# Quantised cross attention in a six-stage transformer kernel: the transposes of 37 of 64 units of probabilities go from TensorE to DMA

## The reference

```python
q = (x @ Wq + bq).reshape(1, B * N, H, hd)            # 512 tokens, 16 heads of 16
kv = (cond @ Wkv + bkv).reshape(1, -1, 2, H, hd)      # 1024 keys
...
q = _fq_sym(q, axis=-1)
k = _fq_sym(k, axis=-1)
v = _fq_sym(v, axis=2)
attn = jnp.einsum('bhqd,bhkd->bhqk', q, k)
attn = jax.nn.softmax(attn.astype(jnp.float32), axis=-1)
attn = _fq_unsigned(attn, axis=-1)                    # rounded to 0..255 steps of its row's maximum
out = jnp.einsum('bhqk,bhkd->bhqd', attn, v)
out = jnp.transpose(out, (0, 2, 1, 3)).reshape(B, N, C)
return out @ Wp + bp
```

## Time and profile before

| what | us |
|---|---|
| three runs | 521.48, 514.76, 516.54; median 516.54 |
| the profiled execution, its whole time | 514.3 |
| its span in the trace | 512.4 |

### The profile page before, as it was taken

How to read it: one execution, slowest core, us unless ns; L and a number is a source line. 1 busy time by engine, 2 the same in 40 slices (tenths; PEclk the granted TensorE clock), 3 DMA queues, 4 the chain that set the end, 5 groups by cost and what they waited for, 6 DMA issues and landing times.

```text
span 512.4 us, 7879 instructions
## 1 busy us (share of the span) xinstructions
PE 447.2 (87%) x2922; PEld 287.7 (56%) x2959; DVE 323.0 (63%) x617; ACT 226.4 (44%) x546; POOL 101.1 (20%) x205
## 2 busy tenths in 40 slices
PE   4977979999996979999974599999999699899994
PEld 1354556666664536756653266666666454455563
DVE  1997368473624258787864789999999464122235
ACT  3331321122222366586520599989898532001000
POOL 6396042424225200000007011111111000000002
PEclk9998988999998879999998589999999989999998
DMA  8930000000000000000000340000000310312121
GB/s 294 317 92 2 0 0 1 0 2 1 1 0 0 1 0 2 2 1 2 1 1 0 123 207 2 1 3 1 2 1 2 117 50 10 123 44 60 41 61 42
DMA packets 12053, 20.63 MB, mean 40 GB/s; under 512 B 1576, under 2 KB 8552, under 8 KB 11688
## 3 DMA queue, kind: packets, MB, share of 16 engines
q1 hardware_dynamic: 12016, 20.14, 11.6%
HBM read 19.48 MB, written 0.66 MB: 39 GB/s over the span
## 4 chain that ended last, share of the span: by engine, by line
PE 72%; DVE 14%; ACT 6%; issue 6%; DMA 1%; POOL 1%; POOLq 0%; SPq 0%; DVEq 0%; ACTq 0%
PE ps L641 23%; PE ps L791 6%; PE ps L1043 5%; PE ps L830 5%; PE ps L841 4%; PE ps L755 4%; PE ps L940 4%; PE ps L960 4%; PE ps L949 4%; PE ps L762 4%; DVE area_a L1381 2%; ACT area_b L572 2%; PE ps L860 2%; PE ps L824 2%; DVE stats L1130 2%
## 5 line engine op out<-in xcount | busy, mean ns | idle before, releaser
L1381 DVE CUSTOM_DVE_ANT_0 area_a<-ps,zero,small 128x1024 f32<-128x1024 f32 x64 | 80.0, 1272 | 1.3 <-PE ps L940 1.3
L572 ACT ACTIVATE area_b<-area_a,small 128x1024 int16<-128x1024 f32 x64 | 72.9, 1142 | 5.9 <-POOL small L451 5.7
L553 ACT ACTIVATE area_a<-ps,small 128x256 f32<-128x256 f32 (+1 forms) x128 | 51.8, 434 | 31.1 <-DVE small L1273 28.8
L641 PE MATMUL ps<-xT_odd,area_a 128*128 128x512 f32 x128 | 58.3, 602 | 0.0
L400 POOL TENSOR_SCALAR var_eps<-meanvar 128x1 f32<-128x1 f32 x24 | 5.9, 245 | 239.5 <-DVE meanvar L1131 239.1
L1448 DVE TENSOR_TENSOR area_b<-ps,area_b 128x512 f32<-128x512 f32 x16 | 11.0, 690 | 52.8 <-ACT area_b L616 52.8
L949 PEld LDWEIGHTS ps<-ident_b,area_b 128*128 128x128 bf16 x512 | 34.0, 99 | 17.5 <-ACT area_b L572 5.3
L940 PE MATMUL ps<-area_b 128*128 128x512 bf16 x107 | 35.9, 405 | 7.5 <-DVE small L1381 3.5
L960 PE MATMUL ps<-area_a,area_b 128*32 128x128 bf16 x512 | 40.1, 222 | 1.0 <-ACT area_a L590 0.8
L1273 DVE TENSOR_REDUCE small<-ps 128x4 f32<-128x1024 f32 (+1 forms) x24 | 29.3, 1222 | 18.3 <-PE ps L830 18.1
L949 PE MATMUL ps<-ident_b,area_b 128*128 128x128 bf16 x512 | 40.0, 222 | 0.8 <-ACT area_b L572 0.7
(11 more groups left out here) (245 smaller groups left out, 789.5 us busy)
## 6 DMA issues: line engine op xcount, KB each, us to landing
area_a<-in_w_up_dram SPq DMA_DIRECT2D x1, 4096.0 KB, 13.6
area_b<-gates_out SPq DMA_DIRECT2D x16, 256.0 KB, 3.0
area_a<-in_w_down_dram SPq DMA_DIRECT2D x1, 2048.0 KB, 8.2
area_b<-in_idx_row_dram SPq DMA_DIRECT2D x1, 1024.0 KB, 7.5
ctxT<-in_ctxT_dram SPq DMA_DIRECT2D x1, 1024.0 KB, 9.5
ctx_tok<-in_ctx_dram SPq DMA_DIRECT2D x1, 1024.0 KB, 12.6
w_qkv<-in_w_qkv_dram SPq DMA_DIRECT2D x1, 768.0 KB, 6.2
xT_even<-in_xT_dram SPq DMA_DIRECT2D x1, 512.0 KB, 3.9
```

The source lines that it names most:

```text
L553: a = act.activation(p1[:, n % 2, x * nk * P:(x + 1) * nk * P], scores1(n)[:, x * nk * P:(x + 1) * nk * P], ACT.Exp, bias=nmx1[:, n % 2, x ...
L572: act.activation(px[:, u % PX, :], sx[:, u % 3, :], ACT.Exp, bias=nbx[:, u:u + 1], accum_out=zx[:, i, h:h + 1]).then_inc(sem("px_ready"), 1)
L641: mm = pe.matmul(dst, lhsT(c), rhs(c), start=start and c == 0, stop=stop and c == DC - 1, **kw)
L1381: dve.tensor_tensor_reduce(sx[:, u % 3, :], bank(2 * (u % 2), 2), zero[:].broadcast_to([P, B * M]), qsc[:, u // HX, u % HX:u % HX + 1], LO ...
```

## The change

37 of the 64 units, the ones whose conversion is DVE's, are no longer transposed by PE. SP issues one `dma_start_transpose` for each of them. It reads `px` in SBUF and writes `turned`, also in SBUF, which has three buffers of int16 and a semaphore for each. DVE then converts from `turned` and no longer from PSUM. The 27 units of ACT keep their path.

- `pTx` gets four buffers, two of them in another area, and a buffer is free again when `apply` of unit u-4 is done.
- On PE, `apply` is three units behind the transposes (before: one). On DVE, the conversion is one unit later in the order: maximum of u+3, then conversion of u.
- The exponential of unit u waits for the landing of the transfer of unit u-3 where that unit is one of the 37 (`px_turned`).
- Steps at the end of a tile (`turn_z`, `spread_z`, `project`, `normalise`, `add`, `norm_scale`, `evac_sums`, `evac_z`) come two or three units later.
- The semaphores `x_ready1` to `x_ready6` become one, `x_ready`, that counts on, and `xT_ready` likewise.

```diff
@@ -54,7 +54,7 @@
 SHARE = ((1, 3, 5), 7)
 TURN_AT = 1
 VALUES_AT = (5, 11)
-NORM_AT = 11
+NORM_AT = 14
 
 
 def build(nc, t, out):
@@ -216,7 +216,9 @@
         zx, rzx = tiny([TT, HX]), tiny([TT, HX])
 
         sx = carve("a", DC * E1 * 2 * HE, [3, B * M])
-        pTx = carve("a", DC * E1 * 2 * HE + 3 * B * M, [2, KT * P], BF16)
+        pTx = [carve(where, at + k * KT * P // 2, [KT * P], BF16)
+               for where, at in (("a", DC * E1 * 2 * HE + 3 * B * M), ("b", 26 * N)) for k in range(2)]
+        turned = carve("b", 11 * N, [3, KT * P], I16)
 
         w_up = carve("a", 0, [DC, 2, E1 * HE])
         w_down = carve("a", DC * E1 * 2 * HE, [NG, D])
@@ -250,10 +252,22 @@
 
             return u % SHARE[1] in SHARE[0]
 
+        def before5(u, by_act):
+
+            return sum(by_scalar(k) == by_act for k in range(u))
+
+        def px_turned(eng, u):
+
+            if by_scalar(u):
+                eng.wait_ge(sem("pTx_ps"), before5(u + 1, True))
+            else:
+                n = before5(u, False)
+                eng.wait_ge(sem(f"turned_{n % 3}"), 16 * (n // 3 + 1))
+
         def pTx_ready(eng, u):
 
             by_act = by_scalar(u)
-            eng.wait_ge(sem("pTx_act" if by_act else "pTx_dve"), sum(by_scalar(k) == by_act for k in range(u + 1)))
+            eng.wait_ge(sem("pTx_act" if by_act else "pTx_dve"), before5(u + 1, by_act))
 
         items1 = [(i, c, hh, gp) for i in range(TT) for c in range(DC) for hh in range(1 + i % 2) for gp in range(2)]
         first1 = [next(n for n, x in enumerate(items1) if x[0] == i) for i in range(TT)] + [len(items1)]
@@ -320,6 +334,16 @@
                 sp.wait_ge(sem("qTx_ps"), HX // 2)
                 load("w_up", w_up.rearrange("p c k h -> p (c k h)"), t["w_up"])
 
+                for u in range(TT * HX):
+                    if not by_scalar(u):
+                        n = before5(u, False)
+                        sp.wait_ge(sem("px_ready"), u + 1)
+                        if n >= 3:
+
+                            sp.wait_ge(sem("pTx_dve"), n - 2)
+                        sp.dma_start_transpose(out=turned[:, n % 3, :].rearrange("p (k q) -> p k q", k=KT),
+                                               in_=px[:, u % PX, :]).then_inc(sem(f"turned_{n % 3}"), 16)
+
                 sp.wait_ge(sem("px_ready"), TT * HX)
                 sp.wait_ge(sem("ox_ps"), TT * HX)
                 load("w_down", w_down, t["w_down"].rearrange("(g p) d -> p g d", p=P))
@@ -335,7 +359,7 @@
                     sp.dma_start(gate_rows[:, g % 4, :], rows).then_inc(sem(f"gate_rows_{g % 4}"), 16)
 
             for i in range(TT):
-                sp.wait_ge(sem(f"x_ready{STAGES}"), i + 1)
+                sp.wait_ge(sem("x_ready"), nth(STAGES, i))
                 sp.dma_start(out[i * P:(i + 1) * P, :], x_tok[STAGES % 2][:, i, :]).then_inc(sem("out_done"), 16)
             sp.wait_ge(sem("out_done"), 16 * TT)
 
...
@@ -568,14 +592,14 @@
                     act.wait_ge(sem("biasx_ready"), u + 1)
                     if u >= PX:
 
-                        act.wait_ge(sem("pTx_ps"), u - PX + 1)
+                        px_turned(act, u - PX)
                     act.activation(px[:, u % PX, :], sx[:, u % 3, :], ACT.Exp, bias=nbx[:, u:u + 1],
                                    accum_out=zx[:, i, h:h + 1]).then_inc(sem("px_ready"), 1)
                     if u and by_scalar(u - 1):
                         evac_px(u - 1)
-                    if h == 1 and i:
+                    if h == 4 and i:
                         evac_sums(i - 1)
-                    if h == 4 and i:
+                    if h == 6 and i:
                         evac_z(i - 1)
                 if by_scalar(TT * HX - 1):
                     evac_px(TT * HX - 1)
@@ -583,11 +607,12 @@
                 evac_z(TT - 1)
 
             def evac_px(u):
-                act.wait_ge(sem("pTx_ps"), u + 1)
-                if u >= 2:
-                    act.wait_ge(sem("ox_ps"), u - 1)
-
-                act.activation(pTx[:, u % 2, :], bank(4 + u % 2).bitcast(I16), ACT.Copy).then_inc(sem("pTx_act"), 1)
+                n = before5(u + 1, True)
+                act.wait_ge(sem("pTx_ps"), n)
+                if u >= 4:
+                    act.wait_ge(sem("ox_ps"), u - 3)
+
+                act.activation(pTx[u % 4], bank(4 + n % 2).bitcast(I16), ACT.Copy).then_inc(sem("pTx_act"), 1)
 
             def evac_sums(i):
 
...
@@ -942,11 +967,14 @@
                     mm.then_inc(sem("sx_ps"), 1)
 
                 def turn(u):
+                    if not by_scalar(u):
+                        return
+                    n = before5(u + 1, True)
                     pe.wait_ge(sem("px_ready"), u + 1)
-                    if u >= 2:
-                        pTx_ready(pe, u - 2)
+                    if n > 2:
+                        pe.wait_ge(sem("pTx_act"), n - 2)
                     for k in range(KT):
-                        mm = pe.transpose(bank(4 + u % 2).bitcast(BF16)[:, k * P:(k + 1) * P],
+                        mm = pe.transpose(bank(4 + n % 2).bitcast(BF16)[:, k * P:(k + 1) * P],
                                           px[:, u % PX, k * P:(k + 1) * P].bitcast(BF16), ident_b[:])
                     mm.then_inc(sem("pTx_ps"), 1)
 
@@ -957,7 +985,7 @@
                     c, pair = divmod(h // 2, P // PAIR)
                     dst = bank(6 + i % 2)[pair * PAIR:(pair + 1) * PAIR, c * P:(c + 1) * P]
                     for k in range(KT):
-                        mm = pe.matmul(dst, ivh[:, k * HX + h, :], pTx[:, u % 2, k * P:(k + 1) * P],
+                        mm = pe.matmul(dst, ivh[:, k * HX + h, :], pTx[u % 4][:, k * P:(k + 1) * P],
                                        start=h % 2 == 0 and k == 0, stop=h % 2 == 1 and k == KT - 1)
                     mm.then_inc(sem("ox_ps"), 1)
 
@@ -982,22 +1010,22 @@
                 pe.wait_ge(sem("in_stage5"), 4 * 16)
                 for u in range(3):
                     scores(u)
-                for u in range(units + 1):
+                for u in range(units + 3):
                     if u + 3 < units:
                         scores(u + 3)
                     if u < units:
                         turn(u)
-                    if u > HX and u % HX == 3:
+                    if u > HX and u % HX == 5:
                         turn_z(u // HX - 1)
-                    if u > HX and u % HX == 5:
+                    if u > HX and u % HX == 7:
                         spread_z(u // HX - 1)
-                    if u > HX and u % HX == 7:
+                    if u > HX and u % HX == 9:
                         project(u // HX - 1)
-                    if u % HX == 1 and u > 2 * HX:
+                    if u % HX == 3 and u > 2 * HX and u < units:
 
                         pe.wait_ge(sem("res5_ready"), u // HX - 1)
-                    if u:
-                        apply(u - 1)
+                    if u >= 3:
+                        apply(u - 3)
                 turn_z(TT - 1)
                 spread_z(TT - 1)
                 project(TT - 1)
...
@@ -1134,7 +1162,7 @@
 
                 dve.wait_ge(sem("rstd_ready"), nth(n, i))
                 TS(x_tok[n % 2][:, i, :], res[:, i, :], meanvar[:, i, 0:1], rstd[:, i:i + 1],
-                   ALU.subtract, ALU.mult).then_inc(sem(f"x_ready{n}"), 1)
+                   ALU.subtract, ALU.mult).then_inc(sem("x_ready"), 1)
 
             def norm(n, residual):
 
@@ -1383,11 +1411,11 @@
                                              mxx[:, u:u + 1]).then_inc(sem("maxx_ready"), 1)
 
                 def evacuate(u):
-                    dve.wait_ge(sem("pTx_ps"), u + 1)
-                    if u >= 2:
-                        dve.wait_ge(sem("ox_ps"), u - 1)
-
-                    dve.tensor_copy(pTx[:, u % 2, :], bank(4 + u % 2).bitcast(I16)).then_inc(sem("pTx_dve"), 1)
+                    px_turned(dve, u)
+                    if u >= 4:
+                        dve.wait_ge(sem("ox_ps"), u - 3)
+
+                    dve.tensor_copy(pTx[u % 4], turned[:, before5(u, False) % 3, :]).then_inc(sem("pTx_dve"), 1)
 
                 def invert_z(i):
                     dve.wait_ge(sem("px_ready"), HX * (i + 1))
@@ -1407,18 +1435,18 @@
                 units = TT * HX
                 maximum(0)
                 maximum(1)
-                for u in range(units):
+                for u in range(units + 1):
                     if u + 2 < units:
                         maximum(u + 2)
-                    if not by_scalar(u):
-                        evacuate(u)
-                    if u >= HX:
+                    if u and not by_scalar(u - 1):
+                        evacuate(u - 1)
+                    if u >= HX and u < units:
                         i = u // HX - 1
                         if u % HX == 1:
                             invert_z(i)
-                        if u % HX == 6:
+                        if u % HX == 9:
                             normalise(i)
-                        if u % HX == 8:
```

(1 more changed line is left out.)

26 lines of the change are left out of this document (13 added, 13 removed).

## The result

The changed kernel took 532.81 us, median of four runs (531.0 to 536.33), against 515.65 for the kernel before. The ratio is **1.036, 95% interval 1.028 to 1.044**: slower by about 17 us. The ratio is one of means and leaves out one execution of the kernel before (521.48 us) which ran in a slower state of the chip, so it is larger than the quotient of the two medians. On another chip, in a later group of runs, the ratio was 1.029 (1.024 to 1.035). The profiled execution has a span of 531.8 us, 19.4 more than before.

A forecast was written before the change was run, and what follows sets the result against it. No engine alone was taken to bound the loop (PE, DVE, ACT over 93% full). 306.7 + 128.9 + 1.23 + 5.15 + 7.68 = 449.7 us for the stage's end, +39.2; with 514.3 and 2.2 about 555 us, range 518 to 640.

The forecast's parts named there:

- the sign: Whole kernel: slower than before, chance 0.83; about 555 us against a median of 516.5.
- the three places of the loss: Start: exponential of unit 3 at 306.7 for 298.94; loop: 2.15 us a unit for 1.70; end: L for 0.72.
- the term L: From the exponential's end until `turned` can be read: between 3.0 and 7.3 us, taken as 5.15.
- everything else: Part of the gate rows' 3.0 us landing that is not service: 2.2 us, beside some 0.8 of service.
- the prediction's own formula: Loop through the landing: seven units take at least 2L + 4.74 us, overtaking the old pace from L = 3.6.
- The pace: Loop over the units: 2.15 us for a unit at L = 5.15, against 1.70 before.
- The ceiling of the gain: Loop from unit 3 to 63: can shrink only to ACT's 95.4 us, at most 6.5 us or 1.3%.
- The start: First transfer queues behind the 4 MB w_up: exponential of unit 3 at 306.7 us in place of 298.94.
- The end: After unit 63's exponential: L replaces the 0.72 us before its conversion; the last norm still ends 7.68 us later.
- The clock: TensorE's half clock at the start may last longer through waiting: nothing in the sum, 3 us in the range.
- the rival with L = 3.0 (524): Transfers land like a plain copy, service 0.8, engines keep 1.70 us a unit: +7.8, 524 us; chance 0.22.
- The conversion: DVE's conversion reading SBUF instead of PSUM: 0.69 us taken as the value, 414 ns as the lower bound.

The follow-up runs named there:

- late conversion: Changed kernel with DVE's conversion of unit u one unit later, after the maximum of u+4 instead of u+3: 525.31 us, ratio 1.019.
- The mended kernel: Changed kernel with w_up in 16 pieces, DVE's conversion one unit later, four px buffers, last three units on PE: 511.7 us, ratio 0.984; again 511.64 us, 0.988.

## Why the prediction was wrong

**What was right**: the sign, the three places of the loss, and ACT as the bound once the rest is mended. **The step that failed** is the term L, the landing. It read: "Nothing in the trace prefers an end; I take the middle, service 2.95 and L = 5.15 us". Measured were 1.63 us of service and a landing of 3.1. Two of its parts were sized wrong. The number of pieces was right (1056, against 1024), but each was charged 79 ns, the mean of a queue whose packets hold 1.7 KB: packets of 256 bytes took 25 ns. And the 2.2 us of "everything else" were 1.5, for the measured service with those 2.2 would have made 3.8. That one value carried 27 of the 39 us through the loop, and some 2 more at either end.

By the prediction's own formula an L of 3.1 gives (6.2 + 4.74) / 7 = 1.56 us a unit, under the 1.70 of before: on average the loop no longer sets the pace, and units 3 to 59 took 1.73. The formula says that a landing under 3.6 us costs nothing there, and that is not so either. With the same order and no transfers they took 92.1 us, so the landings cost 4.8, in single waits of DVE of up to 1.1 us each.

Point by point:

- **The pace**: 2.15 forecast, 1.73 measured for units 3 to 59. The formula is sound where the landing is as long as was assumed: 2.12 by it and 2.21 measured when every transfer was issued twice. In the changed kernel what holds is DVE's order (late conversion, 4.0 us); a fourth buffer of px changed nothing by itself.
- **The ceiling of the gain**: I had seen that ACT leaves 6.5 us at most, of the 101.9 from unit 3 to unit 63. The mended kernel took 98.4 and 98.1 in its two traces, which is 3.5 to 3.8 of them, and the kernel with all units on PE 100.3. The changed kernel took 107.0. DVE's conversions, shorter by 37 x 0.26 = 9.7 us in all, came back as waits for landings, 8.5 us from 306 to 396 us.
- **The start**: +7.8 forecast, +6.8 measured from w_up's issue. The time was near, the reason only half right: "into the same queue behind it" is not what counts. With w_up on another queue the transfer landed as late.
- **The end**: L in place of 0.72 us, 4.4 forecast, 2.9 measured, as the landing is shorter.
- **The clock**: counted at nothing, with 3 us in the range and only for the start. It was low at the other end: 1.7 us in the last tile's steps and 3.7 in stage 6, by the two terms that were gone in the trace with the last units on PE. Of the 3.5 us between units 59 and 63, 1.7 are there without any transfer too; the other 1.8 lie around the stretch where the clock was at 0.65, and no run takes them apart. This is why the time is not that of the rival with L = 3.0 (524) either: 7.8 us by that rival's sum, and some 9 us of these three on top of it.
- **The conversion** from SBUF: 0.43 us, the lower bound; 0.69 was taken.
- **Issuing a transfer**: 1.23 us, not the 0.5 of a plain one; SP had room for it.
- **PE's busy share** of the loop was 83% (75.1 of 90 us) and not 60%. The pace hardly changed, and a unit kept 1.44 us of PE, not the 1.2 of the prediction, which had subtracted the 23 us of transposes from a busy time that lacked 21 matmuls.

The Trainium skill's sentence that transposing DMAs are as fast as regular ones (Advanced Engine Details and Errata, X-Bar Transpose) agrees with the landing, 3.1 us against 3.0 for the same bytes, though not with SP's issue, 1.23 us against 0.51. The 1309 ns of the Trainium skill for a 128x128 block (VectorE: DVE Perf Modes, The three transpose paths) doesn't carry over to eight blocks in one transfer: 3.1 us in all, and not the 10.5 estimated from that page.

The transfer of unit 62 landed 4.8 us after its issue (411.12 to 415.9) instead of 3.1. Unit 63's, issued 2.04 us behind it, isn't what held it up: five pairs in the loop were issued as closely, and landed after 3.1 us. What the trace does show is a load of instructions beside it. The queues from 413.5 to 415.2 us (packets, MB, share):

```profile
q1 hardware_dynamic: 610, 0.15, 97.3%
q8 instruction: 1, 0.02, 3.4%
```

This packet of 16 KB took one of the 16 engines 0.93 us. Behind the start, each of the five landings over 3.3 us in the changed kernel (3.5 to 4.8) has such a packet of 8 or 16 KB at work before it landed. Not every such packet made a landing late, and no experiment tried it, so the cause is likely but not shown.

## What to carry to other kernels

When the cost of a new kind of transfer is unknown, separate what scales with bytes, with packets and with neither before taking a middle: a mean price per packet is a price for packets of the mean size. Then look for what is queued behind the wait for it on each engine. One unit more of distance on DVE was worth about as much as moving the load that stood in the way. And compare with a kernel that has the new order without the new path: against the kernel before, the loop looked free of loss, and it wasn't. A path that is hidden in the middle of a loop still shows at both ends of it: give the last units the shortest path, and keep large loads out of the way of the first.

## What the runs showed of the hardware

- A transposing transfer of 256 KB from SBUF to SBUF: 3.0 to 3.1 us from issue to landing, 1.23 us of SP to issue it, 1056 packets of 25 ns, 1.63 us of each of 16 engines. With w_up under way the second one kept SP at its issue for 7.27 us, and with w_up on ACT's queue one did for 7.46.
- A 4 MB load delayed a later transfer by the same time from its own queue as from another engine's (15.6 and 15.7 us from its issue to the exponential that waited).
- A packet of the instruction queue (16 KB, 0.93 us of one engine) was at work beside the transfer that landed after 4.8 us instead of 3.1.
- TensorE's granted clock went to half behind a stretch in which PE had worked 0.62 of 4 us, and was still there from 428 to 432 us, after PE had been busy for 3.48 us of 420 to 424 and 2.93 of the next four. In one execution with 2.84 us of work in the same stretch it stayed at full speed until 420 us; in another kernel's, with the same last units on PE and 2.91 us of work from 394 to 398, it was at 0.71 from 400 to 404 and at half in the next four. Behind a wait of 2.1 us ahead of a projection, it was granted at 0.65 from 404 to 408.
- DVE's conversion of 128x1024 from int16 to bf16: 0.69 us from PSUM, 0.43 from SBUF.
